# A token, attention and expert block on one core: where the shifted table copies load, and a new order on four engine queues

## What is computed

```python
h = tok_ref(x, token_W, pe)                       # x: (2, 2048) ids below 128
h = h + attn_ref(layernorm(h), ...)               # D = 64, bias_table of 1023 entries
h = h + ffn_ref(layernorm(h), ...)                # 8 experts, top 2, hidden 128
...
# tok_ref: emb = token_W[id] * (id != 0) + pe[j - pad_num]; a scan over the two rows of x,
#          where a pad (id 1) right after a separator (id 13) is skipped
# attn_ref:
rel_bias = bias_table[coords[None, :] - coords[:, None] + (N - 1)]
attn = softmax(einsum('bnc,bmc->bnm', q, k) + rel_bias) * scale
out = layernorm(einsum('bnm,bmc->bnc', attn, v) @ proj_w + proj_b, ln2_g, ln2_b)
# ffn_ref:
topk_w = softmax(top_k(x_flat @ Wg + bg + bias, 2))
hidden = relu(einsum('td,edh->teh', x_flat, W1) + b1)
y = einsum('teh,ehd->ted', hidden, W2) + b2       # then weighted by the two chosen experts
```

## Time and profile before

| | us |
|---|---|
| runs shown, median of 3 (lowest, highest) | 95.45 (94.38, 95.63) |
| the profiled execution's own time | 94.64 |
| its span, first to last instruction | 92.8 |
| busy in the span: DVE / PE / ACT / POOL | 76.9 / 74.9 / 69.4 / 57.0 |

### The profile page before, as it was taken

How to read it: one execution, slowest core, us unless ns; L and a number is a source line. 1 busy time by engine, 2 the same in 40 slices (tenths; PEclk the granted TensorE clock), 3 DMA queues, 4 the chain that set the end, 5 groups by cost and what they waited for, 6 DMA issues and landing times.

```text
span 92.8 us, 2790 instructions
## 1 busy us (share of the span) xinstructions
PE 74.9 (81%) x996; PEld 48.2 (52%) x1004; DVE 76.9 (83%) x305; ACT 69.4 (75%) x141; POOL 57.0 (61%) x111
## 2 busy tenths in 40 slices
PE   0079799786598599899987999998399989999940
PEld 0035596363264354653656665655056556777930
DVE  6899868958956999799999997999997979479970
ACT  0529999515255598889998899998499998958630
POOL 7021007888848874549580789849895878983410
PEclk9999999999999999999999999999999999999999
DMA  1899200000000000000000000000020001100466
GB/s 18 210 292 345 75 4 0 0 7 0 1 4 0 4 0 7 0 0 0 4 7 0 7 0 0 0 7 0 0 57 0 7 0 25 35 7 0 90 126 131
DMA packets 5919, 3.40 MB, mean 37 GB/s; under 512 B 4914, under 2 KB 5266, under 8 KB 5906
## 3 DMA queue, kind: packets, MB, share of 16 engines
q1 hardware_dynamic: 5394, 2.93, 11.6%
q10 hardware_dynamic: 512, 0.31, 1.8%
HBM read 2.17 MB, written 1.06 MB: 35 GB/s over the span
## 4 chain that ended last, share of the span: by engine, by line
DVE 27%; PE 20%; POOL 20%; ACT 13%; issue 10%; DMA 5%; ACTq 1%; POOLq 0%; DVEq 0%
DMA qkv_sb<-in_qkv_dram 5%; DVE pT L925 5%; POOL rs L523 4%; PE bank L1344 4%; PE bank L1371 4%; POOL half L559 3%; PE bank L1402 3%; PE bank L1353 2%; POOL rs L527 2%; ACT oneh_junk L631 2%; ACT ids_all L603 2%; POOL half L560 2%; ACT hid_lo L691 2%; ACT hid_hi L684 2%; DVE stat L769 2%
## 5 line engine op out<-in xcount | busy, mean ns | idle before, releaser
L684 ACT ACTIVATE hid_hi<-bank,b_down 128x512 f16<-128x512 f32 (+1 forms) x40 | 26.2, 658 | 3.5 <-PE bank L1344 3.1
L691 ACT ACTIVATE hid_lo<-bank,b_col 128x512 f16<-128x512 f32 (+1 forms) x40 | 26.3, 659 | 0.4 <-PE bank L1353 0.4
L1353 PE MATMUL bank<-hid_hi,minus_h 128*128 128x512 f16 (+1 forms) x40 | 14.5, 362 | 2.5 <-DVE prod L1006 1.6
L1344 PE MATMUL bank<-xT,w_hi 128*128 128x512 f16 (+1 forms) x40 | 14.3, 360 | 1.1 <-DVE h_all L952 1.0
L1344 PE MATMUL bank<-xT,w_lo 128*128 128x512 f16 (+1 forms) x40 | 14.2, 358 | 0.0
L1006 DVE TENSOR_TENSOR prod<-bank,comb 128x512 f32<-128x512 f32 x14 | 9.5, 687 | 2.5 <-POOL acc L561 1.5
L559 POOL TENSOR_TENSOR half<-prod 128x256 f32<-128x256 f32 x12 | 8.8, 737 | 2.1 <-DVE prod L1006 1.3
L1353 PEld LDWEIGHTS bank<-hid_hi,minus_h 128*128 128x128 f16 x40 | 3.9, 97 | 11.5 <-ACT hid_hi L684 9.2
L1173 PE MATMUL bank<-toe_hi,oneh_j 128*128 128x512 f16 (+3 forms) x24 | 8.3, 354 | 1.8 <-DVE pT L925 1.8
L1371 PE MATMUL bank<-w_hi,hid_hi 128*128 128x64 f16 x112 | 8.4, 193 | 0.9 <-ACT hid_lo L691 0.6
L1371 PE MATMUL bank<-w_lo,hid_hi 128*128 128x64 f16 x112 | 8.4, 193 | 0.0
(11 more groups left out here) (267 smaller groups left out, 230.9 us busy)
## 6 DMA issues: line engine op xcount, KB each, us to landing
w_sb<-in_w1g_dram SPq DMA_DIRECT2D x1, 516.0 KB, 3.6
hankel<-in_bias_table_dram SPq DMA_DIRECT2D x1, 512.0 KB, 4.4
ids_all<-ids_scratch SPq DMA_DIRECT2D x1, 512.0 KB, 4.5
out_dram<-looked SPq DMA_DIRECT2D x2, 256.0 KB
out_dram<-fin_all SPq DMA_DIRECT2D x3, 128.0 KB
w_sb<-in_w2b_dram SPq DMA_DIRECT2D x1, 260.0 KB, 3.8
vec<-in_vecs_dram ACTq DMA_DIRECT2D x1, 104.5 KB, 4.3
vec<-in_vecs_dram ACTq DMA_DIRECT2D x1, 96.0 KB, 3.5
```

Of the source, the lines that this page charges most:

```text
L684: act.activation(hid_hi[:, k % 2, e, 0:m], bank[n % LBANKS][:, 0:m], ACT.Relu, bias=b1_down[:, e:e + 1], scale=KEEP * HSCALE / (XSCALE * X ...
L691: act.activation(hid_lo[:, k % 2, e, 0:m], bank[n % LBANKS][:, 0:m], ACT.Relu, bias=b1_col[:, e:e + 1], scale=HSCALE / (XSCALE * XSCALE)). ...
L1344: ins = mm(bank[n % LBANKS][:, 0:m], w[:, HID * e:HID * (e + 1)], xT[:, k % 2, 0:m], start=part == 0, stop=part == 1)
L1353: mm(bank[n % LBANKS][:, 0:m], minus_h[:], hid_hi[:, k % 2, e, 0:m], start=False, stop=True, skip_group_check=True).then_inc(s_rest, 1)
```

## The change

The DMAs of `hankel` and of the ids' scratch change places on SP, so that `hankel` comes behind the wait for `s_ids`, and with it behind the first small loads. `w1`, `w2`, `b2` and `ids_early` keep their order behind it.

```diff
             sp.dma_start(table_part[:], ...).then_inc(loads["table"], 16)
-            sp.dma_start(hankel[:], ...).then_inc(loads["hankel"], 16)
             sp.wait_ge(s_ids, 1)
             sp.dma_start(ids_dram..., ids_b[:]).then_inc(loads["scratch"], 16)
+            sp.dma_start(hankel[:], ...).then_inc(loads["hankel"], 16)
             sp.dma_start(w1_sb[:], w1g).then_inc(loads["w1"], 16)
```

The four lists of calls are written in a new order. No step is added, removed or changed inside. The parts that the prediction speaks of:

```diff
 POOL
-rsqrt_hidden(); table_values(); embed_parts(); bias_parts(); rsqrt1(0); skip_values(); value_parts()
+rsqrt_hidden(); table_values(); embed_parts(); skip_values(); rsqrt1(0); value_parts(); rsqrt2(0)
-... part_low(1); part_low(2); rsqrt1(2)
+... part_low(1); bias_parts(); part_low(2); rsqrt1(2)
 ACT
-centre_projection(); late_ids(0); late_ids(1); read_folded(); late_ids(2); late_ids(3); centre_bias()
+late_ids(0); late_ids(1); late_ids(2); centre_projection(); late_ids(3); centre_bias(); read_folded()
-... w1_high(); table_exps(1); pair_exps(); ... score_tile(0); score_tile(1); part_high(0); score_tile(2)
+... w1_high(); pair_exps(); ... score_tile(0); table_exps(1); part_high(0); round_rows(0); squares(1)
-hidden(4, 6); read_look(0); hidden(4, 7); low(4, 7); read_look(1)
+hidden(4, 6); hidden(4, 7); low(4, 7); read_look(0); read_look(1)
 DVE
-row_maxima(); minus_ident(); toeplitz_low(1); skip_masks(); split_exps(); rows_a(0); flat_weights()
-rows_b(0); key_part(0); rows_b2(0); part_low(0); rows_c(0); skip_exps(); rows_d(0); rows_a(1); w1_low()
+row_maxima(); w1_low(); flat_weights(); split_exps(); early_one_hots(); rows_a(0); gate_bias(); key_part(0)
+rows_b(0); rows_b2(0); part_low(0); rows_c(0); toeplitz_low(1); rows_d(0); skip_exps(); rows_a(1)
-... weigh(8); early_one_hots(); weigh(9); choose_a(4)
+... weigh(8); weigh(9); choose_a(4)
-weigh_one(0); add_sixth(); weigh_one(1); add_late(); last_rows()
+weigh_one(0); weigh_one(1); add_sixth(); add_late(); last_rows()
 PE
-second_layer(11); first_layer(4, 4); second_layer(12); first_layer(4, 5); last_layer(1); second_layer(13)
-first_layer(4, 6); last_layer(2); look_up(0); first_layer(4, 7); last_bias(2); last_layer(3); last_layer(4)
-last_layer(5); take_high(EXPERTS * UNITS - 1); last_bias(3); last_layer(6); look_up(1); last_bias(4)
-last_layer(7); look_up(2)
+last_layer(0); first_layer(4, 3); last_layer(1); first_layer(4, 4); second_layer(12); first_layer(4, 5)
+last_layer(2); first_layer(4, 6); second_layer(13); last_bias(2); last_layer(3); first_layer(4, 7)
+last_bias(3); last_bias(4); look_up(0); take_high(EXPERTS * UNITS - 1); last_layer(4); last_layer(5)
+last_layer(6); last_layer(7); look_up(1); look_up(2)
```

More of the change, by code:

```diff
@@ L733, in _ @@
+            read_look(0); read_look(1); read_look(2)
         @block.vector
@@ L1073, in _ @@
-            rows_b(0); key_part(0); rows_b2(0); part_low(0); rows_c(0); skip_exps(); rows_d(0); rows_a(1); w1_low()
-            rows_b(1); rows_b2(1); key_part(1); rows_c(1); choose_a(0); rows_d(1); key_part(2); skip_key()
-            skip_key_rows(); choose_b(0); rows_a(2); choose_a(1); rows_b(2); rows_b2(2); key_part(3); rows_c(2)
-            rows_a(3); choose_b(1); rows_d(2); rows_b(3); rows_b2(3); weigh(0); weigh(1); rows_c(3); choose_a(2)
-            weigh(2); rows_d(3); rows_a(4); choose_b(2); weigh(3); rows_b(4); rows_b2(4); weigh(4); rows_c(4); weigh(5)
@@ L1078, in _ @@
-            choose_a(3); weigh(6); choose_b(3); weigh(7); rows_d(4); weigh(8); early_one_hots(); weigh(9); choose_a(4)
+            constants(); id_rows(); hidden_rows(); hidden_stats(); id_columns(); table_top(); one_hot_rows(0, NQ)
+            table_max(); spread_values(); minus_ident(); late_one_hots(); table_bias(); one_hot_rows(JBLK, 2 * JBLK)
+            one_hot_rows(NQ, JBLK); skip_blocks(); toeplitz_low(0); skip_masks(); values(); penalties(); skip_columns()
+            row_maxima(); w1_low(); flat_weights(); split_exps(); early_one_hots(); rows_a(0); gate_bias(); key_part(0)
@@ new lines, in _ @@
+            rows_b(0); rows_b2(0); part_low(0); rows_c(0); toeplitz_low(1); rows_d(0); skip_exps(); rows_a(1)
+            rows_b(1); rows_b2(1); key_part(1); choose_a(0); rows_c(1); key_part(2); rows_d(1); skip_key()
+            skip_key_rows(); choose_b(0); rows_a(2); choose_a(1); rows_b(2); rows_b2(2); choose_b(1); rows_c(2)
+            key_part(3); rows_a(3); rows_d(2); rows_b(3); rows_b2(3); weigh(0); weigh(1); choose_a(2); weigh(2)
+            rows_c(3); rows_a(4); choose_b(2); rows_d(3); weigh(3); rows_b(4); rows_b2(4); weigh(4); weigh(5)
@@ L1079, in _ @@
+            rows_c(4); choose_a(3); weigh(6); rows_d(4); choose_b(3); weigh(7); weigh(8); weigh(9); choose_a(4)
             choose_b(4); weigh(10); weigh(11); weigh(12); weigh_pair(0); weigh(13); gather_two(); weigh_pair(1)
-            weigh_pair(2); sum_last_pair(); weigh_one(0); add_sixth(); weigh_one(1); add_late(); last_rows()
+            weigh_pair(2); sum_last_pair(); weigh_one(0); weigh_one(1); add_sixth(); add_late(); last_rows()
         @block.tensor
@@ new lines, in _ @@
+            attend(6, 4); first_layer(1, 0); gate(1); first_layer(1, 1); embed(2); first_layer(1, 2); weights(3, 5, 8)
+            first_layer(1, 3); embed(3); first_layer(1, 4); first_layer(1, 5); attend(10, 4); first_layer(1, 6)
+            second_layer(0); turn(2); first_layer(1, 7); second_layer(1); first_layer(2, 0); gate(2); first_layer(2, 1)
+            attend(14, 4); first_layer(2, 2); second_layer(2); first_layer(2, 3); embed(4); first_layer(2, 4)
+            second_layer(3); first_layer(2, 5); second_layer(4); first_layer(2, 6); turn(3); first_layer(2, 7)
```

55 lines of the change are left out of this document (23 added, 32 removed).

## The result

The changed kernel takes 90.42 us in the median (90.11 to 91.11) against 95.0 of the kernel before: a ratio of 0.953, 95% interval 0.943 to 0.963. The profiled execution took 90.22 us with a span of 88.4, against 94.64 and 92.8.

The account below looks back on a forecast made before the run. No engine holds the whole: ACT bounds the full expert stretch, PE the tail. Terms 0.85 + 0.7 + 0.1 + 0 = 1.65 off 94.64 give 93.0; 0.2 added for the median makes 93.2, range 91.6 to 95.8.

Parts of the forecast that it names:

- I keep that time: Front on DVE: `gmax` stays at 15.44 to 16.13, since moved DVE work eats the 1 us the ids gain.
- The loads themselves: Front: `hankel`, issued at about 4.7, lands at 9.1 with 0.75 us of cover; cost 0, ends 0 and 1.4 us.
- the forecast 21.4: Front on DVE: `rows_a(0)` at 21.4 against 20.64, after the maxima and four moved steps; 0.75 us late.
- the turned rows 0.45 sooner: Front, unit 0: turned rows some 0.45 us sooner, as POOL no longer has `bias_parts` ahead of its two powers.
- The debt of 2 us: Front on PE: moved work leaves 2.0 us of debt at the first expert layer, absorbed in gaps waiting for ACT.
- The meeting of `w1_low` with `embed_parts`: Front: DVE's `w1_low` now collides with POOL's `embed_parts`; sum up to 1 us worse if POOL holds first.
- the term of 0.85: Front on PE and ACT: gain at unit 1, its first layer at 38.6 against 39.44.
- bounds 0 and 1.57; I take 0.7: Body: DVE's lead over ACT goes to ACT's 1.57 us wait for `gd` at 66.20; 0.7 us gained.
- a second stall replaces the first: Rival: front's lead is there, the gap before 66.20 stays, the tail takes 0.5 back; 94.3, chance 0.3.
- 0.1 for `early_one_hots`: Body on DVE: the early one-hots leaving 71.81 to about 74 gain 0.1 us, bounds 0 and 0.4.
- The tail's 0: Tail: earlier last expert matmuls balanced by later stores, last store 2.46 behind them; 0, bounds -0.3 and +0.7.
- the gap goes wholly: Rival: the whole 1.57 us wait before 66.20 vanishes, 3.1 us gained in all; 91.5, chance 0.15.

Follow-up runs that it names:

- c0: The kernel before with only the DMA of `hankel` moved behind the ids' scratch store; 93.95 us, ratio 0.987.
- c2: The changed kernel's lists on all engines up to the first hidden activation, then the order of before; 93.79 us, ratio 0.995.
- d4: The changed kernel's lists on all engines through unit 0's expert layer, then the order of before; 92.38 us, ratio 0.975.
- b4: The changed kernel with before's front (calls up to the first hidden activation, and load order) put back; 93.2 us.
- d2: The kernel before with ACT's `choice_exp(2)` moved ahead of `round_rows(3)` and `hidden(2, 3)`; 93.87 us, ratio 0.988.
- d6: The kernel before with both ACT calls moved, `choice_exp(2)` earlier and `choice_exp(3)` later; 93.18 us, ratio 0.987.
- d1: The kernel before with ACT's `choice_exp(3)` moved behind `round_rows(4)` and `hidden(3, 2)`; 95.24 us, ratio 1.005.
- a4: The changed kernel with `early_one_hots` put back behind `weigh(8)` on DVE; 90.38 us.
- c3: The changed kernel with before's order for everything behind unit 3 (the old tail); 90.06 us.

## Why the prediction was wrong

**The front: the wrong step is "I keep that time".** I held `gmax` at 15.44, because DVE's moved work "eats" what the ids gain. It came at 14.40. The calls on DVE that moved ahead (masks, one-hot blocks) cost the maxima nothing: c0, with DVE's old order, has 14.46, and DVE's wait for ACT before `total` is 0.17 us in after and 0.34 in c0. The profile of before showed the cause, a wait of 2.17 us for `qkv_sb` at the first row of ACT's queue, and a DMA share of 5% in the chain; the prediction speaks of neither, and did not ask what was queued behind that wait. The loads themselves cost 0 as forecast: `hankel` took 4.2 us to land from its issue at 4.51, so 8.7, and its reader had not to wait for it. Whether the loads behind it on SP's queue slow it comes out at 4.2 against 4.4: they do not. What I missed was its effect on the small load of the other queue, 4.6 us to landing beside it and 2.7 without. The rule that I had cited from the Trainium skill (DMA: Bandwidth & Descriptors, Queues, rings and completion order), one queue in ring order and a round between queues, bears on both, and the traces agree with both halves; I had applied only the first.

**From the maxima to unit 1.** `rows_a(0)` at 20.16 is the forecast 21.4 less the 1.04 of `gmax` and 0.2: the prices of the moved DVE steps were right in their sum (`flat_weights` took 1.19 for 0.96, `split_exps` 1.49 for 1.79). `rows_a(1)` came at 26.11 for 27.4, the power of unit 1 took 1.01 as forecast, and h of unit 1 ended at 29.07 for 30.45.

But PE reached its first expert matmul at 27.32, not 28.8 (and the third, at 29.13, has no bracket). The prediction had the turned rows 0.45 sooner; with the 1.04 of `gmax` that makes 1.5, and the transposed tile came 2.07 earlier, though h of unit 0 ended at 23.04 in both. Nearly all of it was won ahead of PE. DVE has the input of the second power 0.90 earlier (24.64 to 23.74), as `key_part(0)` no longer follows h, and that much was forecast. POOL, which in before does `skip_values` between its two powers, starts the second at 25.95 there, where DVE waits 0.86 for it, and in after at 23.99, right behind its input. I had given POOL's part as `bias_parts` alone and left out `skip_values`. DVE's `xs` ends 1.8 earlier by both (27.64 to 25.83), and PE, which now turns the tile ahead of `weights(2)`, adds the last 0.3: it turns 0.06 behind `xs` (25.89) and did so 0.33 behind it (27.97).

The debt of 2 us was absorbed as forecast (unit 0 took 9.15 instead of 9.65), and c2 against d4 shows the other side: without the interleaving unit 0 takes 1.7 more. The meeting of `w1_low` with `embed_parts`, which I had put at up to 1 us and left out of the sum, moves the first mark by 0.48, by after against c2, according to how the two meet; what `w1_low` would cost there with no meeting at all, no run shows. Unit 1's first layer was forecast at 38.6 and came at 37.14: the term of 0.85 was 2.30, short by 1.04 of `gmax` and 0.4 behind it.

**The body: "bounds 0 and 1.57; I take 0.7".** The gap went whole, and 0.15 beside it: 1.72. My reason, that DVE's lead over ACT would fill it, was not the mechanism: in c2 and d4 the front's lead is there and the gap is 1.57 all the same, and in b4 the gap is gone without that lead. It was the place of two exponents on ACT (d2, d6). The rival "a second stall replaces the first" is what d1 does, though in another place: the first stall goes, and the wait for POOL's sums grows from 1.12 to 2.20.

**The one-hots and the tail.** 0.1 for `early_one_hots` was nothing (a4: the rest is 27.95 with them back behind `weigh(8)`). The tail's 0 was right: c3's rest with the old tail is 28.02. Its parts were about right too. The last store is issued 2.75 us behind the last expert matmul's end (83.07), for a forecast of 2.46.

**The sum.** By the marks 2.07 + 0.50 + 0.03 + 1.72 = 4.32, against 0.85 + 0.7 + 0.1 + 0 = 1.65. Of the 2.67 that were missing 1.75 lie ahead of the gap (2.60 for 0.85) and 0.92 at it (1.72 for 0.8). The rival "the gap goes wholly" at 91.5 had the right outcome of the second part and the wrong front; with `gmax` at 14.4 it would have been 90.5.

## What to carry to other kernels

Ask of each wait in an in-order queue not only what it costs its engine but what stands behind it and who waits for that: here one early wait for a small load held the ids, and one exponent issued two places late made another engine late a unit further on. A wait that the profile shows can be paid for by a call that shows none, so a cure is tried there and not only by filling the gap; filling the gap alone gave back three quarters. And to price a part of a new order, cut all engines at the same time in the program: one engine's list alone gives a mismatch that was no faster than the old kernel, and up to 4% slower.
